# Two of four accumulations per step added by a DMA, a ring of three states, and the down weights loaded on ScalarE's queue

## The reference

```python
def mixer(x):                       # x: [2, 512, 1024]
    u, gate = split(x @ W_in.T)     # 2048 channels each
    u = silu(causal_conv4(u) + conv_b)
    dt, Bm, Cm = split(u @ Wx.T, [64, 80])          # 64, 16, 16 columns
    dt, Bm, Cm = rmsnorm(dt), rmsnorm(Bm), rmsnorm(Cm)
    delta = softplus(dt @ Wdt.T + dt_bias)
    for t in range(512):            # state: [2, 2048, 16]
        state = exp(delta[t] * A) * state + (delta[t] * u[t]) * B[t]
        y[t] = einsum("bdn,bn->bd", state, C[t])
    return ((y + u * D_param) * silu(gate)) @ W_out.T

def qlinear(x, w):                  # both rounded to 8 bits, one scale per row
    return fake_quant(x, -1) @ fake_quant(w, 1).T

x = x + mixer(layernorm(x))
x = x + fake_quant(layernorm(x), s1, z1) @ fake_quant(ctx, s2, z2)
n = layernorm(x)
x = x + qlinear(silu(qlinear(n, w_gate)) * qlinear(n, w_up), w_down)   # 2752 wide
```

## Time and profile before

| | |
|---|---|
| Runs | 1786.21 us median of 3 (1785.23 to 1790.14) |
| Profiled execution | 1786.35 us, its span 1784.6 us, mean granted clock 0.913 of 2.4 GHz |
| Mixer's step loop, first scan to last | 188.2 to 1188.8 us |
| Feed-forward's first loop | 1431 to 1677 us |
| Busy | PE 1407.0 us (79%), DVE 1363.5 (76%), POOL 970.5 (54%), ACT 911.0 (51%) |
| DMA queue 1 (SyncE's) | 42.8% of 16 engines' span |

### The profile page before, as it was taken

One profiled execution on the slowest core, in us unless ns is written; L12 is line 12 of the kernel. 1 busy time (PEld: TensorE's weight loads), 2 busy tenths in 40 slices (PEclk: granted clock), 3 DMA queues, 4 the chain that ended last, 5 costly groups with the idle time before them and its releaser, 6 DMA issues. The chain is left out here.

```text
span 1784.6 us, 17613 instructions
## 1 busy us (share of the span) xinstructions
PE 1407.0 (79%) x5384; PEld 714.3 (40%) x5384; DVE 1363.5 (76%) x1642; ACT 911.0 (51%) x1314; POOL 970.5 (54%) x794
## 2 busy tenths in 40 slices
PE   6998577778779877587887887888999587677478
PEld 3433333444444444444444444443444233223233
DVE  6675899989999989999989898862674645466584
ACT  1212677677677557677676576541422234344450
POOL 0000979788789778898988888941000012122350
PEclk9999889889899989579999899999999799889699
DMA  7694343442433432436727637635710354533204
GB/s 271 215 357 177 103 130 114 162 142 95 164 139 121 134 112 94 138 109 223 255 82 251 213 110 256 224 137 186 267 48 36 83 139 92 138 92 90 63 0 165
DMA packets 155466, 264.36 MB, mean 148 GB/s; under 512 B 76560, under 2 KB 94096, under 8 KB 149552
## 3 DMA queue, kind: packets, MB, share of 16 engines
q1 hardware_dynamic: 152208, 247.54, 42.8%
q10 hardware_dynamic: 3168, 15.73, 2.3%
HBM read 207.60 MB, written 38.60 MB: 138 GB/s over the span
## 5 line engine op out<-in xcount | busy, mean ns | idle before, releaser
L1031 DVE TENSOR_TENSOR_SCAN hbuf<-decay,hbuf 128x512 f32<-128x512 f32 x512 | 612.0, 1212 | 50.3 <-ACT decay L757 50.3
L757 ACT ACTIVATE decay<-delta,chan_sb 128x512 f32<-128x512 f32 x512 | 348.6, 687 | 318.8 <-DVE hbuf L1031 317.3
L577 PE MATMUL turn<-ident,hbuf 128*128 128x128 f32 x2048 | 348.1, 301 | 205.7 <-DVE hbuf L1031 162.2
L577 PEld LDWEIGHTS turn<-ident,hbuf 128*128 128x128 f32 x2048 | 261.9, 153 | 484.6 <-DVE hbuf L1031 242.2
L1045 DVE SCALAR_TENSOR_TENSOR acc<-turn,pn,acc 128x512 f32<-128x512 f32 x360 | 263.0, 731 | 29.2 <-PE turn L577 27.8
L868 POOL TENSOR_TENSOR hbuf<-du,sx 128x512 f32<-128x512 f32 x172 | 213.1, 1275 | 2.0 <-DMA sx<-bt_scratch 2.0
L868 POOL TENSOR_TENSOR hbuf<-wout,sx 128x512 f32<-128x512 f32 x172 | 213.4, 1277 | 0.4 <-POOL wout L878 0.2
L1724 PE MATMUL bank<-codes,wout 128*128 128x512 bf16 (+1 forms) x704 | 171.1, 407 | 52.6 <-DVE gs L1868 51.6
L889 POOL TENSOR_TENSOR acc<-acc,part 128x512 f32<-128x512 f32 x120 | 153.5, 1280 | 60.2 <-ACT part L767 57.7
L1833 POOL TENSOR_TENSOR hid<-gs,us 128x512 f32<-128x512 f32 (+1 forms) x44 | 55.8, 1269 | 187.2 <-ACT gs L1792 187.2
L559 PE MATMUL bank_g<-wout,codes 128*128 128x512 f32 x256 | 138.9, 630 | 1.0 <-DVE wout L968 1.0
(11 more groups left out here) (206 smaller groups left out, 2123.2 us busy)
## 6 DMA issues: line engine op xcount, KB each, us to landing
wout<-in_woutT SPq DMA_DIRECT2D x48, 512.0 KB, 4.3
sx<-bt_scratch SPq DMA_DIRECT2D x86, 256.0 KB, 3.8
codes<-in_wg SPq DMA_DIRECT2D x8, 2048.0 KB, 8.9
ubuf<-u_scratch SPq DMA_DIRECT2D x16, 1024.0 KB, 5.8
wout<-in_w_gate SPq DMA_DIRECT2D x26, 512.0 KB, 4.4
wout<-in_w_up SPq DMA_DIRECT2D x26, 512.0 KB, 4.0
raw_d<-in_w_down SPq DMA_DIRECT2D x8, 1376.0 KB, 6.3
b_more<-bt_scratch SPq DMA_DIRECT2D x42, 256.0 KB, 3.5
```

The source lines that it names most:

```text
L577: last = pe.transpose(turn[t % 2][:, j * P:j * P + P], hbuf[:, s % 4, j, t * P:t * P + P], ident[:, :])
L757: act.activation(decay_bank[q % 2][:, :], delta[:, G % 2, j, :], ACT.Exp, scale=a_col(GD * (G % GROUPS) + j, n)).then_inc(dA_done, 1)
L1031: dve.tensor_tensor_scan(h, decay_bank[q % 2][:, :], h, 0.0, ALU.mult, ALU.add).then_inc(scan_done, 1)
```

## The change

In the mixer, tiles t = 2 and 3 (where n is at least 1) are now scaled by ACT into `part`, which holds both tiles of a step in each of its two slots. POOL adds nothing itself any more: it issues one DMA per step that adds the 128x1024 part to `acc` in SBUF (`accum_op`). The semaphore `part_added` now counts the landing of that DMA, by 16. As before, the next addition waits on POOL until the one before has been done; here that is the landing. ACT's writes to a slot wait for the landing two parts back. To make room, `hbuf` holds three states instead of four.

In the feed-forward, the loads of the down weights are issued on ACT's queue, `plain_d` follows `codes_d` at the same chunk with the next tile's load behind it, and the tiles' maxima stand at chunks 0, 3, 6, 9, 12, 15, 18, 21.

```diff
+HB = 3
-        hbuf = sb("hbuf", [P, 4, GD, L])
+        hbuf = sb("hbuf", [P, HB, GD, L])
-        part = sb("part", [P, 2, GD * P])
+        part = sb("part", [P, 2, TT - TT // 2, GD * P])
...
-        ZT = TT - 1
+        ZT = TT // 2
         def moved(s, tt):
-            return tt == ZT and s % N >= 1
+            return tt >= ZT and s % N >= 1
...
+        def part_count(s, tt):
+            return ZT * (moved_count(s) - 1) + tt - ZT + 1
...
@@ turn_state @@
                 elif s >= 1 and moved(s - 1, t + 2):
-                    pe.wait_ge(part_done, moved_count(s - 1))
+                    pe.wait_ge(part_done, part_count(s - 1, t + 2))
@@ turn_y @@
-                    pe.wait_ge(part_added, (N - 1) * (G + 1))
+                    pe.wait_ge(part_added, 16 * (N - 1) * (G + 1))
@@ scaled_state, on ACT @@
-            def scaled_state(s):
+            def scaled_state(s, tt):
...
                 if k >= 3:
-                    act.wait_ge(part_added, k - 2)
+                    act.wait_ge(part_added, 16 * (k - 2))
...
@@ ACT's loop over the steps @@
                     for j in range(2, GD):
                         decay(s, j)
+                    if s >= 1 and moved(s - 1, ZT):
+                        scaled_state(s - 1, ZT)
                     quant(2 * s)
...
                     if s >= 1 and moved(s - 1, ZT):
-                        scaled_state(s - 1)
+                        scaled_state(s - 1, ZT + 1)
                     quant(2 * s + 1)
@@ times_b, on POOL @@
-                    if s >= 4:
-                        pool.wait_ge(turned, bank_turn((s - 4) // N, (s - 4) % N, TT - 1))
+                    if s >= HB:
+                        pool.wait_ge(turned, bank_turn((s - HB) // N, (s - HB) % N, TT - 1))
@@ add_part, on POOL @@
-                pool.wait_ge(part_done, k)
+                pool.wait_ge(part_done, part_count(s, TT - 1))
...
-                    pool.wait_ge(part_added, k - 1)
-                a = acc[:, s // N % 2, ZT, :]
-                pool.tensor_tensor(a, a, part[:, k % 2, :], ALU.add).then_inc(part_added, 1)
+                    pool.wait_ge(part_added, 16 * (k - 1))
+                pool.dma_start(acc[:, s // N % 2, ZT:TT, :], part[:, k % 2, :, :], accum_op=ALU.add).then_inc(part_added, 16)
@@ feed-forward @@
-        wd_at = {c: t for t, c in enumerate((0, 3, 6, 9, 11, 14, 17, 20))}
+        wd_at = {c: t for t, c in enumerate((0, 3, 6, 9, 12, 15, 18, 21))}
...
@@ SyncE: load_wd and its calls are taken out @@
                     turn_wd(wd_at[c - 2])
-                    if wd_at[c - 2] + 1 < JT:
-                        load_wd(wd_at[c - 2] + 1)
@@ ACT @@
+            def load_wd(t):
+                if t >= 1:
+                    act.wait_ge(wd_plain, NP * t)
+                act.dma_start(raw_d[:, :], w_down[t * P:t * P + P, :]).then_inc(wd_load, 16)
+
+            load_wd(0)
...
                 if c - 1 in wd_at:
+                    t = wd_at[c - 1]
                     for m in range(NP):
-                        codes_d(wd_at[c - 1], m)
-                if c - 2 in wd_at:
+                        codes_d(t, m)
                     for m in range(NP):
-                        plain_d(wd_at[c - 2], m)
+                        plain_d(t, m)
+                    if t + 1 < JT:
+                        load_wd(t + 1)
```

More of the change, by code:

```diff
@@ L102, in mixer @@
         x_view = [hbuf[:, i // 2, 2 * (i % 2):2 * (i % 2) + 2, :].rearrange("p a t -> p (a t)")
-                  for i in range(TOK // P)]
+                  for i in range(2 * HB)] + [part[:, i, :, :].rearrange("p a t -> p (a t)") for i in range(2)]
         RAWS = TOK // P
@@ L576, in turn_state @@
                 for j in range(GD):
-                    last = pe.transpose(turn[t % 2][:, j * P:j * P + P], hbuf[:, s % 4, j, t * P:t * P + P], ident[:, :])
+                    last = pe.transpose(turn[t % 2][:, j * P:j * P + P], hbuf[:, s % HB, j, t * P:t * P + P], ident[:, :])
                 last.then_inc(turned, 1)
@@ L758, in decay @@
                                scale=a_col(GD * (G % GROUPS) + j, n)).then_inc(dA_done, 1)
-            def scaled_state(s):
+            def scaled_state(s, tt):
                 G, n = s // N, s % N
                 k = moved_count(s)
-                act.wait_ge(turned, bank_turn(G, n, ZT))
+                act.wait_ge(turned, bank_turn(G, n, tt))
                 if k >= 3:
-                    act.wait_ge(part_added, k - 2)
+                    act.wait_ge(part_added, 16 * (k - 2))
                 c = R + N + n
-                act.activation(part[:, k % 2, :], turn[ZT % 2][:, :], ACT.Copy,
-                               scale=pn[:, G // GROUPS, ZT, c:c + 1]).then_inc(part_done, 1)
+                act.activation(part[:, k % 2, tt - ZT, :], turn[tt % 2][:, :], ACT.Copy,
+                               scale=pn[:, G // GROUPS, tt, c:c + 1]).then_inc(part_done, 1)
             def gate_copy(G, j):
@@ L848, in _ @@
                         gate_copy(G, j)
-            scaled_state(STEPS - 1)
+            for tt in range(ZT, TT):
+                scaled_state(STEPS - 1, tt)
             for j in gate_copies(NG - 1, N):
@@ L867, in times_b @@
                     pool.wait_ge(du_done, GD * G + j + 1)
-                pool.tensor_tensor(hbuf[:, s % 4, j, :], du[G % 2][:, j, :], b_row[s % 3], ALU.mult).then_inc(dbu_done, 1)
+                pool.tensor_tensor(hbuf[:, s % HB, j, :], du[G % 2][:, j, :], b_row[s % 3], ALU.mult).then_inc(dbu_done, 1)
             def times_u(G, j):
@@ L1029, in scan @@
                 dve.wait_ge(dbu_done, q + 1)
-                h = hbuf[:, s % 4, j, :]
+                h = hbuf[:, s % HB, j, :]
                 dve.tensor_tensor_scan(h, decay_bank[q % 2][:, :], h, 0.0, ALU.mult, ALU.add).then_inc(scan_done, 1)
@@ L1678, in turn_wd @@
                 sp.dma_start(wdT[:, 0:OC, t * P:t * P + P], code_d[:, :], transpose=True).then_inc(wd_turned, 16)
-            def load_wd(t):
-                if t >= 1:
-                    sp.wait_ge(wd_plain, NP * t)
-                sp.dma_start(raw_d[:, :], w_down[t * P:t * P + P, :]).then_inc(wd_load, 16)
             def load_x2(i):
@@ L1692, in store @@
                 sp.dma_start(out[i * P:i * P + P, :], res[i % 2]).then_inc(out_stored[i % 2], 16)
-            load_wd(0)
             for c in range(OC):
```

4 lines of the change are left out of this document (2 added, 2 removed).

## The result

The changed kernel takes 1829.74 us (median of 4 runs, 1828.19 to 1836.37), the kernel before 1785.72 in the same session: ratio 1.0249, 95% interval 1.0218 to 1.0279. It is 44 us slower; 1738 was forecast. Of the profiled executions (span 1827.9 against 1784.6) the mixer ends 66.5 us later, the middle part takes the same 189.4 us, and the feed-forward is 23.2 us shorter (359.5 to 336.3).

The account below looks back on a forecast made before the run. DVE was taken to bound the mixer's loop, the down weights' single buffer the feed-forward's first loop. Mixer -64 + 7 + 25 + 4 + 7 = -21, feed-forward -27: 1786 - 21 - 27 = 1738 us; range 1692 to 1800.

Parts of the forecast that it names:

- What bounds the kernel: Mixer's loop: DVE is the limit, busy 916 of 1001 us, POOL, PE and ACT close behind; shortest step after, 5.78 us.
- ACT's term, +25: Mixer: 33 steps where ACT is the limit gain nothing and lose 0.65 us more, at most 43 us; 25 taken.
- DVE's gain: Mixer: DVE loses 120 additions of 0.65 us, 78 us; outside the loaded stretches 99 x 0.65 = 64 us are gained.
- L = 6.0: Mixer: an adding DMA takes 6.0 us from issue on POOL to landing, 5.0 + 1.0; no step can be shorter.
- rival 1: Mixer: the chain of additions is the limit, L above 7.8 us; at 8.8 the kernel takes 1877 us; chance 0.22.
- The four short-step microseconds: Mixer: L costs only in runs of 5.78 us steps, 6.0 - 5.78 in perhaps 20 steps, 4 us.
- `turn_y`, +7: Group starts: `turn_y` waits for the last part's landing, but DVE waits for ACT's tables anyway; 1 us for each of 7.
- The loaded stretches, +7: First halves of groups 5 to 7: 143 us of DMA work plus 21 additions of 2.4 make 193 against 186, 7 us longer.
- The ring, 0: Mixer: three states instead of four take one step of lead from POOL; costed at nothing.
- The end of the loop, 0: Mixer loop's end: 13 us of cover between the last addition on POOL and `turn_y`, so nothing.
- The feed-forward, -27: Feed-forward: tile 31.3 to 28.1 us, 22 us over seven distances plus 6.1 behind the last; -27 taken, ends -15 to -32.
- ACT and DMA load eat the gain: Mixer: ACT and the DMA load take all of DVE's gain, the mixer stays, 1759 us; chance 0.15.

Follow-up runs that it names:

- tenth: The sixth's kernel with the third tile of steps 1 to 15 neither scaled by ACT nor added by anyone; 1720.70 us, 0.9641 of the kernel before.
- sixth: Changed kernel with the DMA adding only 16 columns of one tile, all issues and waits kept; 1742.24 us, 0.9769 of the kernel before.
- first: Kernel before with only the changed kernel's feed-forward, mixer as before; 1763.69 us, 0.9876 of the kernel before.
- second: Changed kernel with `turn_y`, and the sums, gates and stores behind it, one step later; 1801.67 us, 1.0080 of the kernel before.
- third experiment: Changed kernel with the load of `wg` two steps later, `turn_y` unmoved; 1811.17 us, 1.0140 of the kernel before.
- eighth experiment: Changed kernel with late `turn_y`, late load of `wg` and three slots of `part` together; 1799.03 us, 1.0079 of the kernel before.
- fourth: Changed kernel with three slots for `part` instead of two, so ACT waits for the addition three back; 1828.46 us, 1.0236 of the kernel before.
- seventh: Changed kernel with POOL adding both tiles itself in one 128x1024 operation instead of the DMA; 1756.12 us, 0.9837 of the kernel before.
- ninth: Changed kernel with DMA additions in groups 0 to 3, POOL's own in 4 to 7, and the late `wg` load; 1775.03 us, 0.9951 of the kernel before.
- fifth: Kernel before with a ring of three states instead of four, nothing else; 1786.36 us, 1.0008 of the kernel before.
- eleventh: Kernel before with `plain_d` right behind `codes_d` and tiles three chunks apart, load still on SyncE; 1760.74 us, 0.9863 of the kernel before.

## Why the prediction was wrong, step by step

- **What bounds the kernel** was read rightly: DVE, with the others close. Its 120 additions went at 0.65 us each. The short step came out at 5.77 against 5.78.
- **ACT's term, +25**: 21.5 measured (tenth against sixth).
- **DVE's gain** was taken at full price, 0.65 for each of 99 steps outside the loaded stretches, with ACT's waits as the only deduction. Of 78 us only 43 come out with the data and ACT's second tile taken away (tenth against first). Steps that other work sets do not shorten. This alone made the forecast some 20 us too good.
- **L = 6.0**: the median is 6.2 from issue to landing, with 0.88 of issue on POOL (1.0 was taken); the chain of additions (rival 1) never set the average step. But L was one number for all places, and it runs from 4.5 to 11.4: medians of 8.2, 8.8 and 7.9 in the first halves of groups 5 to 7. There, and at the groups' starts, rival 1's sign, POOL idle for its own DMA, did appear. The four short-step microseconds were the wrong place to price it.
- **`turn_y`, +7: failed.** I let ACT's table load cover it with 1 us left per group. PE waits 50.7 us in 7 places. I had the last addition issued at 9.5 us and landed at some 15.5. The issue is so in groups 1 to 3, but it lands at 19.7 to 21.4: I had priced the landing at L = 6 without asking what is issued beside it, SyncE's 2048 KB of `wg`. In groups 4 to 7 the addition before it meets that load, the last waits for it on POOL, and lands at 24.4 to 26.4. And I had counted only DVE's cover, not that PE's queue stands with all transposes in it, and that its clock falls. Cured by the second or the third experiment, it is worth 28 and 19 us.
- **The loaded stretches, +7: failed.** 21 additions at 2.4 us against free time: I let the DMA engines run full and asked only for what exceeded that. The additions took 2.74. By the windows' shares the engines worked 145 us in the three first halves before (0.81 x 62.1 + 0.79 x 61.7 + 0.75 x 61.5) and 202 after (0.91 x 76.4 + 0.87 x 78.5 + 0.87 x 74.0). The 57 between are 21 x 2.74. So 17 of the 44 us by which these halves grew are work beyond their old length (202 against 185), and the other 27 are time in which the engines were not full: 228.9 - 202. I had let the free time of a whole half be filled to the last microsecond. Their average share of 0.88 is this same 202 / 228.9 and no limit of the engines. Stretches of group 5 were full (columns of the earlier trace rows; a share over 1 comes from packets counted where they start):

```profile
842.00:862.00 20.00, 9.87 (x30) 6.17 (x30) 8.52 (x9) 11.37 (x14) 10.64 (x9) 0.75 1.04 349
880.00:920.00 40.00, 28.91 (x97) 15.28 (x98) 27.79 (x29) 21.57 (x34) 27.76 (x24) 0.83 0.98 292
```

In between the share was 0.69 (860 to 880), and in the eighth experiment the same halves had 0.92, 0.92 and 0.90 and were no shorter. What stood still meanwhile: POOL for the landing before, 22.8 us in 9 of the 24 steps; PE for `woutT`, 18.1, and for `turn_y`'s addition, 18.1. Taking away `turn_y`'s wait (second) or ACT's (fourth) brought nothing back here; taking away the data did (sixth, seventh, ninth).
- **The ring, 0**: right for the kernel before (fifth). In the changed kernel POOL stands 81.6 us for it, but DVE has no wait for POOL's products. **The end of the loop, 0**: the mixer's blocks show nothing else there.
- **The feed-forward, -27**: -22 to -23. The tile is 28.8 us, not 28.1, and the seven distances between maxima add up to 199 us after 217, 18 less instead of 22. The fall of PE's clock that I had in the range did not come: the granted clock of the block is 0.89 before and after. The cause of the gain was mis-told: I gave the queue of SyncE as much weight as the copy's place, and the eleventh shows that moving the copy does it all. The Trainium skill (DMA: Bandwidth & Descriptors, "Issuing engines are not separate DMA queues") says that the saving is only the issuing sequencer's time and usually small. The eleventh agrees: its 3.4 us lie under cover, and nothing is lost by them.
- **The adding DMA's rate.** The runs agree with the Trainium skill (Collectives: The Full Stack, "The bandwidth ceiling: the fold count and why AG ≠ RS ≠ AR"), which says of a ReduceScatter that its add needs two source reads: here it is 5.2 us of 16 engines per MB against 3.1, a factor of 1.7.

In sum, the mixer was forecast at -21 and came at +66. The terms: 35 us of DVE's 78 that do not come out instead of 14, ACT 21.5, and the addition's data 87.5, of which 60 lie in groups 5 to 7, 22 in groups 1 to 4, and the rest in group 0. The rival with the right place, "ACT and DMA load eat the gain" (1759), lacked the size.

What stays open: how the 60 us of groups 5 to 7 divide between the chain of additions (each issued only when the one before has landed, which no experiment with the full data takes away) and the later landing of `woutT` and `wg` on full DMA engines. No run here separates them.

## What to carry to other kernels

Work moved to the DMA engines is paid in the stretch it falls in: add the new transfers' time to what that stretch already moves, and do not count on the gaps being filled: here 202 us of work took 229, since the stretch is full in some places and waits in others. Then look at what is issued beside a transfer for which the head of an in-order queue waits, since it lands with its neighbours, and at whether transfers wait for each other's landing. And of two edits for one wait, try each alone: here moving the copy ended it, and the queue was not needed.
